# A graph kernel with and without the one-hot gather of every eighth chunk on TensorE

## The reference

```
for _ in range(2):                                      # layer 0, two message steps
    edge_input = concat([h[ei], h[ej], edge_attr])      # 128 + 128 + 32 features an edge
    m_ij = relu(edge_input @ We1 + be1) @ We2 + be2
    h = h + segment_sum(m_ij, ej)
x = layernorm(x + h + bias)
h = x @ weight.T                                        # layer 1: weighted graph convolution
out = segment_sum(h[src] * (dinv[src] * ew * dinv[dst])[:, None], dst) + bias
x = layernorm(relu(out) + x)
```

## Time and profile before

| | us |
|---|---|
| median of three runs | 2679.2 |
| span of the profiled execution | 3568.7 |
| profiled execution outside its span | not listed |
| POOL busy | 1843.2 |
| PE busy | 2679.8 |
| DVE busy | 1482.6 |
| ACT busy | 685.7 |

### The profile page before, as it was taken

How to read it: one execution, slowest core, us unless ns; L and a number is a source line. 1 busy time by engine, 2 the same in 40 slices (tenths; PEclk the granted TensorE clock), 3 DMA queues, 4 the chain that set the end, 5 groups by cost and what they waited for, 6 DMA issues and landing times.

```text
span 3568.7 us, 72128 instructions
## 1 busy us (share of the span) xinstructions
PE 2679.8 (75%) x24750; PEld 2452.1 (69%) x24750; DVE 1482.6 (42%) x3796; ACT 685.7 (19%) x1685; POOL 1843.2 (52%) x1781
## 2 busy tenths in 40 slices
PE   3788877787777777977777878777878767776775
PEld 2687766777677766766676767677767666666765
DVE  3443333433443433443333333333333655554564
ACT  2010000000000000110000100000000355555553
POOL 3455545454655454266565655556656454444442
PEclk7777778778878777677888787788787877877777
DMA  5222222222222222322222222222222211111111
GB/s 123 65 77 73 67 67 69 68 70 69 72 70 75 65 70 63 90 75 77 77 71 75 75 75 75 69 72 77 75 75 75 59 36 30 33 31 31 31 30 36
DMA packets 186116, 233.28 MB, mean 65 GB/s; under 512 B 77720, under 2 KB 137231, under 8 KB 185876
## 3 DMA queue, kind: packets, MB, share of 16 engines
q0 software_dynamic: 56512, 115.85, 12.0%
q1 hardware_dynamic: 122324, 112.13, 11.6%
q10 hardware_dynamic: 7168, 4.09, 0.4%
HBM read 221.77 MB, written 10.12 MB: 65 GB/s over the span
## 4 chain that ended last, share of the span: by engine, by line
PE 72%; issue 22%; another core or an unknown queue 2%; DVE 2%; DMA 2%; ACT 0%; DVEq 0%; SPq 0%; ACTq 0%
PE ps L580 30%; PE ps L590 14%; PE ps L576 14%; PE ps L677 6%; PE ps L667 5%; PE ps L587 1%; DMA gat<-dst_row 1%; DMA cbase_dram<-cint 1%; PE ps L753 1%; PE ps L749 0%; PE ps L690 0%; PE ps L608 0%; DVE node_b L1079 0%; DVE stats L1388 0%
## 5 line engine op out<-in xcount | busy, mean ns | idle before, releaser
L515 POOL DMA_INDIRECT gat<-p_dram,idx x1438 | 1504.4, 1046 | 1245.5 <-DVE msg L1183 768.0
L580 PE MATMUL ps<-x,node_a 128*128 128x128 bf16 x4900 | 608.8, 253 | 187.2 <-issue 185.7
L855 ACT ACTIVATE msg<-msg 128x512 f32<-128x512 f32 x404 | 253.6, 630 | 2411.3 <-DVE msg L1183 2127.7
L580 PEld LDWEIGHTS ps<-x,node_a 128*128 128x128 bf16 x4900 | 472.4, 116 | 232.6 <-issue 229.1
L576 PE MATMUL ps<-rhs,lhs 96*128 96x128 f32 x3232 | 532.5, 320 | 123.8 <-issue 105.8
L580 PE MATMUL ps<-adj,node_a 128*128 128x128 bf16 x2450 | 554.2, 253 | 93.2 <-issue 92.6
L1183 DVE TENSOR_TENSOR msg<-ps,gat 128x512 f32<-128x512 f32 x404 | 275.6, 688 | 826.2 <-remote 408.9
L576 PEld LDWEIGHTS ps<-rhs,lhs 96*128 96x128 f32 x3232 | 475.6, 227 | 144.7 <-issue 129.2
L580 PE MATMUL ps<-x,adj 128*128 128x128 bf16 x4000 | 476.5, 252 | 118.9 <-issue 118.6
L515 POOL DMA_INDIRECT gat<-z_dram,idx x328 | 326.0, 994 | 391.9 <-PE ps L590 192.5
L580 PE MATMUL ps<-adj 128*128 128x128 bf16 x2000 | 444.9, 252 | 53.9 <-issue 53.8
(11 more groups left out here) (151 smaller groups left out, 2517.2 us busy)
## 6 DMA issues: line engine op xcount, KB each, us to landing
dbc<-dst_row SPq DMA_DIRECT2D x202, 256.0 KB
lhs<-eaT SPq DMA_DIRECT2D x202, 128.0 KB
gat<-p_dram,idx POOLq DMA_INDIRECT x1438
sbc<-src_row SPq DMA_DIRECT2D x202, 64.0 KB
rhs<-q_dram SPq DMA_DIRECT2D x202, 32.0 KB
gat<-z_dram,idx POOLq DMA_INDIRECT x328
idx<-src_g SPq DMA_DIRECT2D x243, 4.0 KB
p_dram<-node_a ACTq DMA_DIRECT2D x12, 256.0 KB, 3.3
```

What stands on the lines that cost most here:

```text
L515: return pool.indirect_dma_start(out=out_, out_offset=None, in_=table, in_offset=bass.IndirectOffsetOnAxis(ap=index, axis=0))
L580: last = nc.tensor.matmul(acc, shot[s][:, t, :], p_part[k][:, t, :], start=False, stop=(t == HI - 1 and k == 2))
L855: nc.scalar.activation(m, m, ACT.Relu).then_inc(relu_done, 1)
```

## The change

The one-hot gather goes. POOL gathers eight chunks in every group of passes 0 and 1, and the loops of all engines become loops over pairs of groups. With it go the split of P into three parts, the loads of `sbc`, the instructions at L1154, L1157, L1159 and L1188, the matmuls at L580, the numbers of the nodes (an iota of POOL at the start), and the counting of rows that stretches needed. Pass 2 is as before but for these counts.

```
-                            for c in range(h * HALF, min((h + 1) * HALF, CH - 1 if own else CH)):
+                            for c in range(h * HALF, (h + 1) * HALF):
                                 rows(gat[s][:, c, :], table, idx[s][:, c:c + 1]).then_inc(rows_in[s][h], 16)
...
-            def pre_products(s, h, gather=False):
+            def pre_products(s, h):
                 for c in range(h * HALF, (h + 1) * HALF):
-                    own = gather and c == CH - 1
-                    acc = ps_pre(s, h)[:, (c % HALF) * P:(c % HALF + 1) * P]
-                    last = nc.tensor.matmul(acc, lhs[s][:, c * P:(c + 1) * P], rhs[s][:, :], start=True, stop=not own)
-                    if own:
-                        for t in range(HI):
-                            for k in range(3):
-                                last = nc.tensor.matmul(acc, shot[s][:, t, :], p_part[k][:, t, :], start=False,
-                                                        stop=(t == HI - 1 and k == 2))
+                    last = nc.tensor.matmul(ps_pre(s, h)[:, (c % HALF) * P:(c % HALF + 1) * P],
+                                            lhs[s][:, c * P:(c + 1) * P], rhs[s][:, :], start=True, stop=True)
...
-                        row = src_row[bass.ds(g * GE + GE - P, P)].rearrange("(a n) -> a n", a=1)
-                        sp.dma_start(sbc[s][:, :], row.to_broadcast([P, P])).then_inc(sbc_in[s], 16)
...
-                    for q, (t0, n) in enumerate(QUADS):
-                        n = min(n, HI - t0)
-                        nc.scalar.copy(p_part[0][:, t0:t0 + n, :], node_a[:, t0:t0 + n, :]).then_inc(part_cut, 1)
...
-                    dve.wait_ge(q_out, 16 * len(QUADS) * (p + 1))
-                    for q in range(len(QUADS)):
-                        left_of(q)
...
-                    dve.wait_ge(part_left, base + 2 * len(QUADS))
-                    dve.wait_ge(p_out, 16 * len(QUADS) * (p + 1))
...
-                        dve.wait_ge(sbc_in[s], 16 * used(p, s, k))
-                        if p > 0 or type(g) is not int or g > 0:
-                            dve.wait_ge(shot_made, n)
-                        V.tensor_scalar(sbc16[:, :], sbc[s][:, :], float(MID), None, ALU.subtract).then_inc(sbc_cut, 1)
-                        dve.wait_ge(sbc_cut, n + 1)
-                        if not own:
-                            V.memset(scratch[:, :], 0.0).then_inc(shot_made, 1)
-                        else:
-                            V.tensor_tensor(shot[s], numbers, sbc16[:, :].unsqueeze(1).to_broadcast([P, HI, P]),
-                                            ALU.is_equal).then_inc(shot_made, 1)
...
-                        if not own and more:
-                            dve.wait_ge(pre_added, 2 * n + 2)
-                            V.memset(gat[s][:, CH - 1, :], 0.0)
```

More of the change, by code:

```diff
@@ L313, in nth, with rows_of, rows_of3, pair @@
             return p * NG + g
[L315 to L321, removed]
-        def groups(eng, step):
[L327 to L341, removed]
+        def rows_of(use):
+            return 16 * HALF * use
+        def rows_of3(i, at, back=0):
+            return i * (16 * HALF * P_TURN // 2) + rows_of(used3(0, at) - back)
+        def groups(eng, step):
+            def pair(k, first):
+                g = 2 * k
+                step(g, 0, k + 1, first)
+                step(g + 1, 1, k + 1, first)
+            pair(0, True)
+            with eng.Fori(1, PAIRS) as k:
+                pair(k, False)
+            step(NG - 1, 0, PAIRS + 1, False)
         def used(p, s, k):
@@ L427, in _, with load @@
                 with sp.If(fast == 1):
-                    def load(g, s, k, first, whole, own, own_next):
+                    def load(g, s, k, first):
                         old = p > 0 or not first
                         if old:
-                            sp.wait_ge(rows_in[s][1], rows_of(s, 1, used(p, s, k) - 1,
-                                                             p * WHOLE[s] + whole - (0 if own else 1)))
+                            sp.wait_ge(rows_in[s][1], rows_of(used(p, s, k) - 1))
                         if not first:
@@ L463, in _ @@
                         turns(sp, load3)
-                        sp.wait_ge(rows_in[0][1], rows_of3(0, 1, TURNS - 1, None, back=1))
+                        sp.wait_ge(rows_in[0][1], rows_of(LAST_USE - 1))
                         sp.dma_start(idx[0][:, :], src_g[NG - 1, :, :]).then_inc(idx_in[0], 16)
@@ L503, in _ @@
                       allow_small_or_imprecise_dtypes=True).then_inc(pool_const, 1)
-            pool.iota(numbers, pattern=[[P, HI], [0, P]], base=-MID, channel_multiplier=1,
-                      allow_small_or_imprecise_dtypes=True).then_inc(pool_const, 1)
             pool.memset(cw[:, :], 0.0).then_inc(pool_const, 1)
             pool.memset(aggT[:, :], 0.0).then_inc(pool_const, 1)
-            pool.wait_ge(pool_const, 9)
+            pool.wait_ge(pool_const, 8)
             pool.affine_select(out=ident[:, :], in_=ident[:, :], compare_op=ALU.not_equal, fill=1.0,
@@ L523, in _, with gather @@
                 with pool.If(fast == 1):
-                    def gather(g, s, k, first, whole, own, own_next):
+                    def gather(g, s, k, first):
                         pool.wait_ge(idx_in[s], 16 * used(p, s, k))
@@ L627, in _, with products @@
                 with pe.If(fast == 1):
-                    def products(g, s, k, own):
+                    def products(g, s, k):
                         n = nth(p, g)
@@ L635, in products @@
                                 pe.wait_ge(pre_added, 2 * (n - 2) + h + 1)
[L636 to L640, removed]
+                            pre_products(s, h).then_inc(pre_mm, 1)
                     def sums(g, s):
@@ L651, in sums, with step @@
                         scatter_products(p, s).then_inc(scat_mm, 1)
-                    def step(g, s, k, first, whole, own, own_next):
+                    def step(g, s, k, first):
                         if type(g) is not int or g < NG - 1:
-                            products(g + 1, 1 - s, k + s, own_next)
+                            products(g + 1, 1 - s, k + s)
                         sums(g, s)
@@ L704, in step3 @@
                         if TURN[at] == "P":
-                            scatter3(n, r % 2, i, at, None if start and r < 2 else adds(i, at))
+                            scatter3(n, r % 2, rows_of3(i, at), None if start and r < 2 else adds(i, at))
                             return
@@ L717, in _ @@
                     if p < 2:
-                        products(0, 0, 1, False)
+                        products(0, 0, 1)
                         groups(pe, step)
@@ L850, in _, with relu @@
                     with act.If(fast == 1):
-                        def relu(g, s, k, first, whole, own, own_next):
+                        def relu(g, s, k, first):
                             for h in range(2):
@@ L1142, in add_window, with one_hots @@
                         V.tensor_tensor(a, a, ps_agg(s), ALU.add).then_inc(agg_added, 1)
-                    def one_hots(g, s, k, own):
+                    def one_hots(g, s, k):
                         n = nth(p, g)
@@ L1169, in scatter_hots, with vector_step @@
                             tally_up(s, g).then_inc(hotw_made, 1)
-                    def vector_step(g, s, k, first, whole, own, own_next):
+                    def vector_step(g, s, k, first):
                         n = nth(p, g)
```

59 lines of the change are left out of this document (10 added, 49 removed).

## The result

The changed kernel takes 2716.5 us (median of four runs, 2712.4 to 2721.4), against 2680.0 for the kernel before on the same chip: ratio 1.0144, 95% interval [1.0119, 1.0168]. It is 36.5 us slower; 2700 was predicted, and the side is the predicted one.

A forecast was written before the change was run, and what follows sets the result against it. POOL's gathers, with DVE's holds among them, were taken to bound passes 0 and 1; 222 - 198 - 3 = +21 us on 2679 gave 2700 us, range 2634 to 2766 us, likeliest case 2685 to 2766.

The forecast's parts named there:

- The bound: In passes 0 and 1, POOL's gathers, with DVE's holds among them, bound the timed runs, at about 10.1 us a group.
- the 890 us: Excess of the profiled span, 3568.7 us, over the 2679.2 us median; taken as PE gaps belonging to that profiled execution.
- Time of the passes before: Passes 0 and 1 in a timed run: 2679 - 156 (outside) - 487 (pass 2) = 2036 us.
- The gather: One more gather on POOL in 178 groups, 1.248 us each, +222 us, all on the path.
- The hold: DVE's one-hot (L1159) delays a POOL gather by 0.75 to 1.48 us, middle 1.115; removing 178 gives -198 us.
- The matmuls removed on PE: 13,350 matmuls, 75 a group, hidden because PE's 7.86 us lies under POOL's 10; removal gives nothing back.
- The start of the passes: Node-table split on ACT and DVE ahead of each pass goes; POOL's first wait in pass 0 may go, -3 us.
- The first: Rival: one-hot holds a gather longer, 1.25 us up, so the change is faster, 2574 to 2674 us; chance 0.24.
- The second: Rival: PE, not POOL, bounds the timed runs before, and an untraced gather is cheaper; 2500 us; chance 0.07.
- The third: Rival: PE at 1.2 GHz throughout, its chain takes POOL's place in passes 0 and 1; about 2900 us; chance 0.06.
- What was to show it: Signs: eight gathers a group at 1.24 us, none over 1.7 us beside a one-hot, passes near 1030 us, PE waiting for relu.

## Why the prediction was right, and where its sizes were off

**The bound** was right: POOL's gathers with DVE's holds. Setting the 890 us aside was right too, and the runs confirm it (2676.9 us of span). The reason given, that the gaps fall on 13,350 matmuls, was not: seven other profiled executions with 75 matmuls a group, the kernel before's own among them, are as long as their timed runs. The span did drop by 854 us, but not through the change.

**Time of the passes before.** Worked out: 2036 us for 0 and 1. Measured: 2036.9. That it fits so closely is luck, for two guesses in it were off and cancelled: pass 2 takes 453.5 us, not 487, and 186.5 us, not 156, lie outside the three.

**The gather,** 1.248 us and +222 us: right (217.7 by difference, 1.22 to 1.28 each). It was also right that all of it lies on the path.

**The hold** was the mis-sized term: "178 x 1.115 = -198 us". By the two profiles 177.3 us went, 1.00 us a one-hot. These 21 us are the miss, less some 4 us of other small differences: 2716.5 instead of 2700. The middle of 0.75 and 1.48 was not a bad guess (with a PE at half clock it is 1.11), but the gathers were read one by one. The 0.75 us at 571.13 had a first part in the gather ahead of it: the 1.45 us at 569.37, which the prediction put down to L1149, began 0.80 us before that one-hot:

```profile
570.17 1.83 DVE L1159 TENSOR_TENSOR node_a<-khots,sbc 128x3200 bf16<-128x3200 f16 x1
```

Together the two lost 0.51 + 0.75 = 1.26 us, as start + 0.45 us has it. The lower end of the range, 0.75, was thus no whole hold, and how often each length comes can't be read from four holds.

**The matmuls removed on PE,** "hidden and their end gives nothing back": this came true for the change as made, since zeros in their place move the changed kernel by no more than the noise. The reason given doesn't carry further, though. The matmuls were hidden, yet their removal costs 11 to 21 us while the one-hot is there, and the zeros take it back. It isn't a charge of its own on top of the row above: by the sums of over-time it is why the holds before were 1.00 and not 1.11 us. By which chain of waits a slower PE moves the one-hot's start (SP's queue waits for PE's products, and DVE for SP's dbc) wasn't tried and stays open.

**The start of the passes:** -3 us forecast, 4.7 us of POOL's waits went.

**The rivals.** The first needed a hold over 1.25 us in the mean; there are such holds, but the mean is 1.00. The second falls with the one-hot made twice (PE unchanged, 167 us gone) and the gather's price. The third had its clock as foreseen (0.51), but not its time. Of that clock the Trainium skill, "TensorE: Matmul & The Clock Gate" (HAM oscillation — how this bites in real kernels), had warned, and the trace agrees (0.51). In the rows above PE waits 2.47 + 0.48 us in a group, and even at 9 us a group (seven gathers) POOL waits for adds 0.3 us in all.

**What was to show it:** gathers each 1.248 us, passes of 1032.6 and 1044.2 us (1030 forecast), 1.2 us of waits for DVE's adds, and PE waiting for relu (238.6 us for L545) all came. One gather did go over 1.7 us, beside L989 and not beside a one-hot (see the last section).

## What to carry to other kernels

Where POOL issues indirect DMAs without a pause, a long DVE instruction with two inputs in SBUF can be paid for by POOL, so the cheap-looking half of a trade (here a one-hot that saves a gather) must be priced on both engines; moving one input to PSUM made it half as fast and the kernel 6.6% faster. Add up over-time over neighbouring instructions before you size a stall: what one engine loses to another depends on where in its period it is hit. When a profiled execution is far longer than the timed runs, profile again before you explain its waits.

## What the runs showed that was not expected

- Idle multiplications are worth time: 75 matmuls of zeros a group made the kernel without the one-hot's products 14 us faster (2696.0 to 2681.7), by moving when a DVE instruction starts.
- L1149 (one input in SBUF, 0.75 us) holds gathers too, as at 1509.86 above (1.35 instead of 0.94 us); what is left of over-time after the change, 61.9 us, is mostly beside it (33 us where it and the add were met, by the trace). The gathers end as those beside L1159 do: in the changed kernel it held 176 by over 0.05 us, alone or with the add behind it, and 149 of these end 0.81 to 0.82 us after it. So two such inputs were enough for a hold in L1159, but a hold doesn't need them. The adds, with one input in PSUM, hold nothing: 254 gathers that met one alone lost 1 ns in the mean.
- L1030, with two inputs in SBUF, holds little: of 183 gathers that met it alone in the changed kernel, 28 took over 0.05 us too long, 0.07 us in the mean over all. It is a matter of its place, by the trace: each of the 28 times it (0.69 us) began 1.09 to 1.20 us after the start of a gather, in the pause ahead of the next, and that next one ended 0.81 to 0.82 us after it. Nine in ten of the 155 gathers not held met one that began within 0.31 us of a gather's start and was over before the next began. So this short instruction is paid for only where it meets the start of a gather.
- The longest hold left in the changed kernel, met once, is beside L989, which takes 3.68 us and reads two whole tensors in SBUF. That gather, too, ends 0.82 us after the DVE instruction:

```profile
1163.44 3.68 DVE L989 SCALAR_TENSOR_TENSOR xTs<-hT,bias_col,xTs 128x3328 f32<-128x3328 f32 x1
```
```profile
1164.65 3.29 POOL L476 DMA_INDIRECT gat<-p_dram,idx  x1 [0.30 <-issue]
```
